# Attention and MLP kernel on one core: up projections over two token tiles, one transposition of the shifts, local values by tokens

## The reference

```python
q, k, v = (split_heads(xn @ W) for W in (Wq, Wk, Wv))
k_c, v_c = blocks_of_16(k) @ Wck, blocks_of_16(v) @ Wcv           # compressed branch
out_c = softmax(q @ k_c.T / 4, blocks that have ended) @ v_c
top_idx = top_k(logits_c, 4)                                      # selected branch
out_s = softmax(q @ k[tokens of the 4 blocks].T / 4) @ v[same]
out_l = softmax(q @ k.T / 4, at most 32 tokens back) @ v          # local branch
out = (gates[..., 0:1] * merge(out_c) + gates[..., 1:2] * merge(out_s) + gates[..., 2:3] * merge(out_l)) @ Wo
mlp = silu(xn @ Wg + bg) * (xn @ Wu + bu) @ Wd + bd
w = silu(xn @ down_embed[idx]) * softmax(scores);  experts = w @ up_embed[idx]
y = x + out + mlp + experts
```

## Time and profile before

| | us |
|---|---|
| median of 3 runs | 1507.11 (1507.01 to 1509.83) |
| the profiled execution | 1507.87 |
| its span in the trace | 1506.1 |
| busy: TensorE / its weight loads | 1420.1 / 1044.1 |
| busy: VectorE / ScalarE / GpSimd | 1187.8 / 928.4 / 919.1 |

### The profile page before, as it was taken

How to read it: one execution, slowest core, us unless ns; L and a number is a source line. 1 busy time by engine, 2 the same in 40 slices (tenths; PEclk the granted TensorE clock), 3 DMA queues, 4 the chain that set the end, 5 groups by cost and what they waited for, 6 DMA issues and landing times. The chain is left out here.

```text
span 1506.1 us, 43877 instructions
## 1 busy us (share of the span) xinstructions
PE 1420.1 (94%) x14960; PEld 1044.1 (69%) x14960; DVE 1187.8 (79%) x4544; ACT 928.4 (62%) x1684; POOL 919.1 (61%) x845
## 2 busy tenths in 40 slices
PE   6899679999999999999999999999999999999978
PEld 4566447777777777777777777777777777777657
DVE  5444288888888888888888888898888888888812
ACT  3766336666666666666666666666666666666641
POOL 4655356666666666666666666666666666666620
PEclk8999879999999999999999999999999999999989
DMA  6556942221111122222111122212222222222027
GB/s 186 205 183 211 274 73 53 52 51 45 47 45 47 50 51 51 51 51 50 47 46 46 47 50 49 48 48 51 51 51 51 51 51 51 65 51 53 9 95 234
DMA packets 217147, 113.74 MB, mean 76 GB/s; under 512 B 128872, under 2 KB 211224, under 8 KB 217112
## 3 DMA queue, kind: packets, MB, share of 16 engines
q1 hardware_dynamic: 216304, 112.88, 27.3%
q10 hardware_dynamic: 808, 0.42, 0.2%
HBM read 73.08 MB, written 40.16 MB: 75 GB/s over the span
## 5 line engine op out<-in xcount | busy, mean ns | idle before, releaser
L1150 POOL TENSOR_TENSOR sumxy<-xy 128x1024 f32<-128x1024 f32 x128 | 240.7, 1901 | 0.0
L1393 DVE TENSOR_REDUCE bmax<-q_bank 128x32 f32<-128x512 f32 (+3 forms) x512 | 219.9, 481 | 16.5 <-PE q_bank L1633 15.4
L1240 ACT ACTIVATE pts<-k_bank 128x512 f32<-128x512 f32 (+2 forms) x384 | 177.4, 490 | 42.0 <-PE k_bank L1668 41.2
L1494 DVE SCALAR_TENSOR_TENSOR mw<-sumxy,c,ex 128x1024 f32<-128x1024 f32 x128 | 176.0, 1394 | 1.5 <-issue 0.8
L1633 PE MATMUL q_bank<-ko,qo 96*128 96x512 bf16 (+3 forms) x512 | 142.9, 306 | 24.6 <-DVE bmax L1393 22.6
L1116 POOL TENSOR_TENSOR pad<-pad 128x1 f32<-128x1 f32 x32 | 6.2, 193 | 256.4 <-DVE top L1412 256.4
L1615 PE MATMUL f_bank<-xt,wfu 128*128 128x128 f32 x1024 | 162.3, 281 | 0.0
L1174 POOL TENSOR_TENSOR cw<-cw,mw 128x1024 f32<-128x1024 f32 x64 | 150.8, 2356 | 6.6 <-ACT mw L1264 1.6
L1615 PE MATMUL f_bank<-xt,wfg 128*128 128x128 f32 x1024 | 150.3, 279 | 0.0
L1615 PEld LDWEIGHTS f_bank<-xt,wfu 128*128 128x128 f32 x1024 | 139.4, 191 | 11.5
L1264 ACT ACTIVATE mw<-mw,erec 128x1024 f32<-128x1024 f32 x128 | 145.7, 1139 | 0.0
(11 more groups left out here) (211 smaller groups left out, 3340.1 us busy)
## 6 DMA issues: line engine op xcount, KB each, us to landing
qo<-s_qs SPq DMA_DIRECT2D x192, 64.0 KB, 2.2
ko<-s_ks SPq DMA_DIRECT2D x186, 64.0 KB, 2.2
s_qs<-parts SPq DMA_DIRECT2D x8, 768.0 KB, 4.7
s_ks<-parts SPq DMA_DIRECT2D x8, 768.0 KB, 6.3
s_v<-vo SPq DMA_DIRECT2D x8, 544.0 KB, 3.0
vv<-s_v SPq DMA_DIRECT2D x32, 136.0 KB, 2.3
vw<-s_v SPq DMA_DIRECT2D x64, 68.0 KB, 2.5
xin<-in_L_attn_x_dram SPq DMA_DIRECT2D x8, 512.0 KB, 6.9
```

Of the source, the lines that this page charges most:

```text
L1150: done("sum_done", g_.tensor_tensor(sumxy[:, h, :, :], xy[:, 0, h, 0:XK, None].broadcast_to([P, XK, KEYS]), xy[:, 1, h, None, :].broadcast ...
L1240: last = s.activation(pts[:, h, OFFS[j]:OFFS[j] + n], bank[:, 0:n], ACT.Exp)
L1393: last = v.tensor_reduce(bmax[:, i, h, 0:n], Q.bank(job)[:, o:o + n * BLK].rearrange("p (n j) -> p n j", j=BLK), AX.X, ALU.max)
L1494: done("mw_done", v.scalar_tensor_tensor(mw[:, h, :], sumxy[:, h, :, :].rearrange("p a b -> p (a b)"), c8[:, h, 7:8], ex[:, h % 2, :], ALU ...
```

## The change

Five things change.

1. **Up projections.** A step computes half of the hidden columns for both token tiles of the pair (256 tokens, new tile `xp`, loaded with the near loads of the odd unit) instead of all of them for its own tile: 16 products of 256 columns in place of 32 of 128. `mlp_down` takes the same 8 products, 4 for each token tile, and the bank `y` is filled over two steps, read by VectorE once in a pair. The store, the load of `xb` and `result_in` on GpSimd also come once a pair with twice the size.
2. **Shifts.** The step begins with `head_shifts(t)`: four products turn the shifts of all four heads at once into bank a, and ScalarE copies it in four pieces of 32 rows, one after the other, ahead of the tanh of `w0`. For this head h has its shift rows at 32h in `qo` and its one-hot at 32h in `ko`; the parts take the other three groups. `queries` and `window` now use all 128 rows, so the shift rows must be zero when the unit is first used: they are loaded from a tensor of zeros in memory.
3. **Loads.** `load_parts` becomes 4 loads of zeros (32 KB), 16 of queries and 16 of keys (16 to 48 KB) instead of 12 of 64 KB.
4. **Local values by tokens.** The small products are turned round (weights pT, 17 moving columns), so that tokens lie in the partitions; ScalarE's copy and the four transposes (`tl`) go. They are done in two halves, after the last `queries`, around the last part of `mlp_down`, where before they stood after the third head.
5. **VectorE.** `expert_sum` stands in front of `key_marks` and no longer after the third head's maxima. Some semaphores are merged.

On TensorE, where one step ends and the next begins, before: w0 (wdn,xt) heads the step, and one head's shifts come within the gate's products.

The diff, cut to its core:

```diff
+    s_zero = dram("s_zero", [32, T], BF16)
...
-            SP3 = 96
+            PARTS = ((0, 0), (2, 0)), ((0, 1), (0, 2)), ((1, 0), (1, 1))
...
+            xp = sb("xp", [P, 2, 2 * P])
...
-            k_jobs = ["pcT", "co", "a0"]
+            k_jobs = ["a", "pcT", "co"]
             for h in range(HG):
-                k_jobs += [f"s{h}0", f"s{h}1", f"s{h}2"] + [f"a{h + 1}"] * (h < HG - 1) + [("pl0", "pl1", "vl", "tl")[h]]
-            k_jobs += ["vs", "ts"]
+                k_jobs += [f"s{h}0", f"s{h}1", f"s{h}2"] + [f"pl{h}"] * (h < 2)
+            k_jobs += ["vl", "vs", "ts"]
...
+            def part_rows(to, src, which, half):
+                for i, pair in enumerate(PARTS):
+                    lots = [(3, i, i + 1)] + [(i, h0, h1) for h0, h1 in ((0, i), (i + 1, HG)) if h0 < h1]
+                    for quad, h0, h1 in lots:
+                        for n in range(2):
+                            o = 32 * quad + D * n
+                            yield to[o:o + D, half, h0:h1, :], src[pair[n][which]][:, h0:h1, :]
...
                 def load_near(b, g, half):
+                    both = [(xp[:, :, :], row(s_xt, b)[:, :, (g - 1) * P:(g + 1) * P])] if half else []
                     send([(qf[:, half, :], row(qff, b)[g]), (kc[:, half, :], row(kcf, b)[g]),
-                          (xt[:, half, :, :], row(s_xt, b)[:, :, g * P:g * P + P])], near_in[half], N_NEAR)
+                          (xt[:, half, :, :], row(s_xt, b)[:, :, g * P:g * P + P]), *both], near_in[half], N_NEAR[half])
                 def load_parts(b, g, half, keys=True):
                     q, k = row(qs, b)[g], row(ks, b)[g]
-                    pairs = [(to[D * n:D * n + D, half, :, :], src[r])
-                             for to, src, parts in ((qo, q, Q_ROWS), (ko, k, K_ROWS))[:2 if keys else 1] for n, r in enumerate(parts)]
-                    send(pairs, parts_in[half], N_PARTS if keys else N_PARTS // 2)
+                    pairs = [(qo[32 * h:32 * h + 32, half, h, :], s_zero) for h in range(HG)]
+                    pairs += part_rows(qo, q, 0, half)
+                    if keys:
+                        pairs += part_rows(ko, k, 1, half)
+                    send(pairs, parts_in[half], N_PARTS if keys else N_QUERIES)
...
+                        if half:
+                            Y.wait_read(sp, t.round(), "y")
+                            sp.sem_inc(carried, 1)
                         load_late(b, g, half)
...
                 def lead(n):
-                    g_.tensor_copy(ko[SP3:P, :, :, :].rearrange("p a h t -> p (a h) t"),
-                                   onehot[SP3:P, None, :].broadcast_to([P - SP3, 2 * HG, T])).then_inc(key_blocks, 1)
-                    pool.wait_ge(key_blocks, 1)
                     selection(n)
                     candidates(n)
...
-                for n, r in enumerate(K_ROWS):
-                    act.dma_start(ko[D * n:D * n + D, 0, :, :], k_first[r]).then_inc(parts_in[0], 16)
+                for h in range(HG):
+                    act.dma_start(ko[32 * h:32 * h + 32, :, h, :],
+                                  onehot[96:128, None, :].broadcast_to([32, 2, T])).then_inc(key_blocks, 16)
+                for dst, src in part_rows(ko, k_first, 1, 0):
+                    act.dma_start(dst, src).then_inc(parts_in[0], 16)
...
-                def head_shifts(t, h):
-                    K.wait_full(act, t, f"a{h}")
-                    K.released(f"a{h}", s.activation(qo[SP3:P, t.half, h, :], K.bank(f"a{h}")[SP3:P, :], ACT.Copy))
-                def openings(t):
-                    head_shifts(t, 0)
-                    tanh(t, "g0", hidden(0), "th_done")
-                def branch_values(t, k):
-                    job = ("vs", "vl")[k]
-                    K.wait_full(act, t, job)
-                    K.released(job, s.activation(oT[:, k, :], K.bank(job)[:, :], ACT.Copy))
+                def head_shifts(t):
+                    K.wait_full(act, t, "a")
+                    for h in range(HG):
+                        rows = slice(32 * h, 32 * h + 32)
+                        last = s.activation(qo[rows, t.half, h, :], K.bank("a")[rows, :], ACT.Copy)
+                    K.released("a", last)
+                def selected_values(t):
+                    K.wait_full(act, t, "vs")
+                    K.released("vs", s.activation(oT[:, :], K.bank("vs")[:, :], ACT.Copy))
...
                 def step(t):
                     n = None if t.tail else t.next()
+                    head_shifts(t)
                     tanh(t, "w0", sw[:, 0:512], "tw_done")
                     block_shares(t)
...
-                    job = ("ts", "tl")[k]
+                    job, w = (("ts", 32), ("vl", VW))[k]
                     K.wait_full(dve, t, job)
-                    bank = K.bank(job)[:, :].rearrange("p (i h w) -> p i h w", i=TT, h=HG)
-                    cf.link(v.reciprocal(rs[:, :, :], bank[:, :, :, D]))
+                    bank = K.bank(job)[:, 0:TT * HG * w].rearrange("p (n w) -> p n w", w=w)
...
+                    expert_sum(t)
+                    if n:
                         key_marks(n)
                     gate(t, 1)
                     if n:
                         for part in range(3):
                             block_max(n, 2, part)
-                    expert_sum(t)
                     if n:
                         unselected(n, now=t)
...
-                    result(t)
+                    if t.half:
+                        result(t)
...
-                        mm(F.bank(f"{name}{j}")[:, :], bias3[:, kind, j, :], tile_of[:, :, :].rearrange("r k t -> r (k t)"),
+                        mm(F.bank(f"{name}{j}")[:, :], bias3[:, kind, t.half, :], tile_of[:, j, :, :].rearrange("r k t -> r (k t)"),
                            start=True, stop=True)
-                    o = P * (4 * j + k)
-                    dst = F.bank(f"{name}{j}")[:, k * P:k * P + P]
-                    for c in range(2):
-                        last = mm(dst, w_[:, c, o:o + P], xt[:, t.half, c, :], start=False, stop=(c == 1),
-                                  skip_group_check=True)
+                    f, c = divmod(k, 2)
+                    o = P * (4 * t.half + 2 * j + f)
+                    last = mm(F.bank(f"{name}{j}")[:, 2 * P * f:2 * P * f + 2 * P], w_[:, c, o:o + P], xp[:, c, :],
+                              start=False, stop=(c == 1), skip_group_check=True)
...
-                def local_values(t):
+                def local_values(t, r):
                     bank = K.bank("vl")
-                    for g in range(T // 32):
-                        for h in range(HG):
-                            rows, k = slice(64 * (h // 2), 64 * (h // 2) + 64), h % 2
-                            last = mm(bank[32 * h:32 * h + VW, 32 * g:32 * g + 32], vw[rows, t.half, g, VW * k:VW * k + VW],
-                                      pT[rows, k, 32 * g:32 * g + 32], start=True, stop=True, skip_group_check=True)
-                    K.filled("vl", last)
+                    rows = slice(64 * r, 64 * r + 64)
+                    for k in range(2):
+                        for g in range(T // 32):
+                            i, q = divmod(g, 4)
+                            o = VW * (HG * i + 2 * r + k)
+                            last = mm(bank[32 * q:32 * q + 32, o:o + VW], pT[rows, k, 32 * g:32 * g + 32],
+                                      vw[rows, t.half, g, VW * k:VW * k + VW], start=True, stop=True, skip_group_check=True)
+                    if r == 0:
+                        done("vl_half", last)
+                    else:
+                        K.filled("vl", last)
...
-                def token_values(t, k):
-                    K.wait_read(pe, t, ("vs", "vl")[k])
-                    job = ("ts", "tl")[k]
-                    K.wait_free(pe, t, job)
+                def token_values(t):
+                    K.wait_read(pe, t, "vs")
+                    K.wait_free(pe, t, "ts")
                     for i in range(TT):
-                        last = tr(K.bank(job)[:, P * i:P * i + P], oT[:, k, P * i:P * i + P], ident[:, :])
-                    K.filled(job, last)
+                        last = tr(K.bank("ts")[:, P * i:P * i + P], oT[:, P * i:P * i + P], ident[:, :])
+                    K.filled("ts", last)
...
+                    K.wait_free(pe, t, "a")
                     for i in range(TT):
-                        last = mm(K.bank(f"a{h}")[SP3:P, P * i:P * i + P], shift_s[:, i, h, :], identb[:, :],
-                                  start=True, stop=True)
-                    K.filled(f"a{h}", last)
+                        last = mm(K.bank("a")[:, P * i:P * i + P], shift_s[:, i, :, :].rearrange("p h n -> p (h n)"),
+                                  identb[:, :], start=True, stop=True)
+                    K.filled("a", last)
...
-                    for f in (2 * part, 2 * part + 1):
-                        mm(Y.bank("y")[:, 0:C], hT[:, f, :], wfd[:, f, :], start=(f == 0), stop=False)
```

(24 more changed lines are left out.)

140 lines of the change are left out of this document (74 added, 66 removed).

## The result

The changed kernel takes 1531.83 us (median of 4 runs, 1531.21 to 1536.03) against 1508.47 for the kernel before beside it (1507.01 to 1512.05): ratio 1.0158, 95% interval 1.0138 to 1.0178. Forecast were 1496 us and a range of 1472 to 1522. It is slower, and outside the range.

A forecast was written before the change was run, and what follows sets the result against it. A ring through TensorE and VectorE was taken as the bound: 10.15 + 10.7 + 17.65 = 38.5 us a step, 0.44 less. Over 31 steps 13.6, with start +4 and end -2 a gain of 11.6: 1496 us, range 1472 to 1522.

The forecast's parts named there:

- Leg 1: TensorE, from the third head's last query rows to the start of VectorE's local maxima: 10.96 us falling to 10.15.
- the ring: Timeline loop through TensorE and VectorE, cut into three legs, said to set the step of 38.94 us.
- The 2.25 us wait for candidates is worth nothing on the ring.: VectorE's 2.25 us wait per step for GpSimd's candidates goes, but stood where TensorE leads, so it gains nothing.
- Leg 2: VectorE, from the start of the local maxima to its third expert product: 10.50 us growing to 10.7.
- The first rival: Front of the step costs what the heads give: Leg 2 at 11.3 us, 1515 us in all; chance 18%.
- Leg 3: VectorE, from third expert product through gate and third head's maxima to its last query rows: 17.48 us growing to 17.65.
- The start: First step, where w0 now waits for the shifts: +4 of a possible 4.8 us.
- the end's -2: Last step, where nothing of a next unit waits: gains TensorE's full 2 us.
- The local values keep their pace: TensorE's local-value products: same pace, 0.0105 us each; the rival had them doubled, +1.3 us a step, 1536 us, chance 7%.
- The loads come in time: SyncE's 36 transfers land before TensorE needs them, 0.6 us left; the rival had them late, 1536 us, chance 9%.
- TensorE's 2.1 us whole: Rival: TensorE's saving of 2.1 us a step comes through whole, 1446 us; chance 8%.
- three signs: Wrong if shift copies exceed 2.4 us, transfers land after TensorE asks, or local values hold TensorE over 2 us.

The follow-up runs named there:

- f1: Changed kernel with VectorE's second hidden product moved ahead of the unselected mask and best pairs: 1512.92 us, ratio 1.003.
- f2: Changed kernel with the unselected mask moved behind the fourth head's maxima on VectorE: 1511.18 us, ratio 1.0017.
- g3: Changed kernel with the local values' two halves around the third part of the down projections, not the fourth; TensorE only: 1511.12 us, ratio 1.0012.
- b1: Kernel before the change with only expert_sum moved early, in front of key_marks: 1500.13 us, ratio 0.9946.
- e1: Changed kernel with expert_sum put back behind the third head's maxima: 1558.97 us, ratio 1.0333.
- f3: f2 with ScalarE copying three heads' shifts ahead of the first tanh and the fourth's behind the fourth expert's exponential: 1493.41 us, ratio 0.9894.
- g2: f3 with ScalarE's block-share copy behind the fourth exponential and the four one-hot loads issued behind the first key-score copy: 1489.05 us, ratio 0.9858.

## Why the prediction was wrong

The forecast was a gain of 11.6 us, the result a loss of 23.4 in the span: 35 us apart. By its own terms:

- **Leg 1: forecast 10.15, measured 10.91; 24 of the 35 us.** The prediction took from leg 1 what TensorE no longer does and kept the rest of the leg as it was ("Leg 1, TensorE"). This is the step that failed: the wait of TensorE for VectorE's hidden product, put at nothing without a reason. Its arithmetic on TensorE's work was right: as soon as the wait is removed, on either engine, leg 1 is 10.05 to 10.14. It did not ask what TensorE would meet when it came earlier to the third part of the down projections; the ring had a second engine within leg 1, 0.7 us away, and the change brought TensorE 2.0 us nearer. f1, f2 and g3 show it.
- **"The 2.25 us wait for candidates is worth nothing on the ring."** In the kernel before that holds for leg 1 (b1: 10.94). In the changed kernel it would have cost (e1), so the early sum was needed, and it is worth 27 us there. What took part of the wait's place, a mask of 1.96 us and not 0.41, was not foreseen. What the early sum gives in the kernel before, 0.5 us in leg 2 through `bsel`, the prediction used only to date the shifts.
- **Leg 2: forecast 10.7, measured 10.91; 6.5 us.** The mechanism, the place and the date of the shifts' product are right (5.85 for 6.0). The term that was mis-sized is the four copies: 3 x 0.49 + 0.59 = 2.06 was read from two ScalarE rows of different lines; four in a row take 2.38. f3 shows that one copy less gives 0.55. The first rival (11.3) lay further off.
- **Leg 3: forecast 17.65, measured 17.57.** Right.
- **The start: forecast +4, measured +8.6; 4.6 us.** The part that was forecast, w0 behind the shifts, is right: from the first local maxima to the block values' product it takes 4.4 us more. Another 2.5 lie ahead of it, between SyncE's first issue in this stage and those maxima (27.0 us for 24.5): the units' first loads, which the prediction left out. The last 1.7 are a stage that begins later (187.4 for 185.7), and that varies: from 187.0 to 193.8 in the kernels with the changed start, from 185.7 to 186.0 in the three with the old one. The key scores are copied 4.2 us later, behind the 20 loads that ScalarE's queue issues first; but with four of these out of the way the maxima hardly came earlier (g2), so this copy is not what holds the start. Which of the loads does was not tested.

```profile
190.16 7.98 ACTq L1266 DMA_DIRECT2D ko<-s_ks  x16
...
198.27 0.60 ACT L1308 ACTIVATE sim<-f_bank 128x512 f32<-128x512 f32 x1 [25.63 <-issue]
```
- **One step, and the end.** The 2.6 us of the 30th step were in no term of the sum. Of the end's -2 about 1.3 came.
- **The local values keep their pace**: 64 from 722.38 to 723.04, 0.0103 each, forecast 0.0105. That rival is out.
- **The loads come in time**: 16 issues take 7.62 and 7.82 us, 0.48 to 0.49 each (forecast 0.466), and TensorE does not wait in front of co. Right, and that rival is out.
- **TensorE's waits for block maxima** were to grow to 2.5 us a step; they are 3.4, as the step is longer and the work was saved in legs 2 and 3 without use. That rival, TensorE's 2.1 us whole, is out too.

Together 23.6 + 6.5 - 2.5 (leg 3) + 4.6 + 2.6 + 0.7 (the end) = 35.5, for the 35.0 to be explained. None of the three signs by which the prediction would know that it was wrong came: the copies took 2.38 us and not over 2.4, the transfers landed in time, the local values held TensorE for 2 x 0.66 us.

What the range missed was not an unknown cost but an unasked question: no rival dealt with VectorE's order in leg 1.

## What to carry to other kernels

When work is taken from an engine, look for the first thing it will ask another engine for and compare two times: when it will come there now, and when the thing is ready. If the engine comes earlier by more than the gap, only the gap is gained there, and the order of the other engine's queue is part of the change. Look in the same way at instructions put in a row ahead of one that is waited for; what needs no early copy goes behind it.

## What the runs showed of the hardware

- **The mask and the pair sums.** The same VectorE instruction (a comparison of 128x512 f32 to bf16) takes 0.41 us alone and up to 1.98 us beside GpSimd. Started 0.21 us after the first pair sum it took 1.96, started 0.82 us after it 1.37: it ends 0.3 us behind that GpSimd instruction. So it does behind another one, in f2:

```profile
712.29 2.35 POOL L1215 TENSOR_TENSOR cw<-cw,sw 128x1024 f32<-128x1024 f32 x1
712.93 1.98 DVE L1473 TENSOR_SCALAR unsel<-struck 128x512 bf16<-128x512 f32 x1
```

- The time is inside the instruction's own length; the profile shows no idle time of VectorE for it. The trace bears out the Trainium skill here, "SBUF — State Buffer", SBUF: two separate sides, which says that VectorE and GpSimd share a port pair as an exclusive lock held for a whole instruction, and that a VectorE instruction takes part in it if it runs in a two-port mode or has two inputs in SBUF. In which mode the mask runs the profile does not show.
- `bsel`, with two inputs in SBUF, is 0.68 us long in b1 and mostly 1.2 in the kernel before. Not every instruction beside a pair sum grows: in f1 the hidden product, with one of its inputs in PSUM, starts at 713.11 beside the sum of 712.89 and takes 0.68, as ever.
- **Copies by ScalarE of 32 rows** take 0.59 us each and 2.38 for four in a row; ScalarE instructions on different banks and tiles start 0.49 apart. Why the four do not overlap I did not test.
